# Four tables that place convolution and attention jobs among feed-forward chunks, laid out anew

## The chip, the cores and the metric

The kernel runs on one core of a Trainium2 chip. The metric is the device time of one launch in microseconds (us): the median of three runs before the change is 751.4, and the three lie between 750.59 and 752.95.

## The reference, cut to what matters

The input has 4 images of 96 channels and 56 x 56 pixels. Each goes through one transformer block:

```
x = x + conv_attention(layernorm over channels of x)
t = x as 3136 tokens of 96 channels
t = t + moe(layernorm(t))

conv_attention: value, query = depthwise 3x3 conv, stride 1;  key, off = the same, stride 2
   offset = w_off2 (gelu(layernorm(off)));  pos = tanh(offset + ref)
   sampled = value read bilinearly at pos (784 places, four neighbours each)
   out = (query^T key * scale) sampled  per head;   y = w_out out
moe: 4 experts, 96 -> 384 -> 96 with gelu, top 2 of a softmax gate:
   out = sum over experts of gate_e * (w2_e gelu(w1_e t + b1_e) + b2_e)
```

## The kernel before

**Two kinds of work share every engine.** The feed-forward part of an image is 84 chunks: 7 groups of 448 tokens, by 4 experts, by 3 slices of 128 hidden units. A chunk is, on PE, a first product in three passes (L762 to L764, fp32r split in high and low parts), a gelu on ACT (L1006), and a second product on PE (L746). PE issues the second product of chunk k-1 behind the first product of chunk k. There are two PSUM banks for first products, so PE can't be more than two chunks ahead of ACT. Three chunks make one output of an expert: DVE scales it by the gate (L1416, tile ye), and POOL adds it to the image (a sum). The first 76 sums are accumulating DMAs that POOL issues (L1480), and POOL waits before each until the sum before it has landed. The first 252 chunks (images 0 to 2) are spread between the convolution and attention jobs of images 1 to 3. The last 84 (image 3) run by themselves at the end, in another form (L782 to L797, L1015, L1443).

**The other kind are the jobs of the image ahead**, a long chain through all engines. For image b, in the order in which PE meets them:

- valT: transposes of the value convolution (L621). DVE has to be through with its nine value taps (L1133). ACT then writes the table of values to memory.
- xT: the next image's pixels to tokens (L529); keyT: the key convolution to samples (L566).
- pad: the next image, normalised, back to channels (L534 to L556). Ahead of it DVE takes the statistics and scales one part of the tokens (L1098), and ACT scales the rest (xn in its table, L831).
- kv (L632): products of keys and sampled values, in four quarters. DVE samples (L1335, L1338) from what POOL gathered from the table (L1469, two gathers for each of eight tiles). A DMA of this kind lands in the tile `big`.
- mix and y (L642, L662): the attention. DVE adds y to the image (L1354), and PE turns the sum to tokens again (x1T, L650).
- offT, offc, offs: the next image's offset convolution, from which DVE and ACT (tanh) derive the places of the gathers.
- x1c (L511): the normalised tokens back to channels, seven jobs. ACT takes the high part (L930), DVE the low part (L1369). Before them ACT scales three groups (x1n), and between them stand the softmax (exp, L939) and the gate (gateT).

DVE issues, in this order of an image: low parts of x1c, the offset normalisation, value and key and query taps, the statistics of the next image, the sampling, the masking of kv, the sums with y, the statistics of the tokens, the gate.

**The order on each engine is written out by hand in four tables.** `CHUNKS_AHEAD` says for each PE job how many chunks PE has to have issued before it. `GELUS_AHEAD` says the same of the gelus on ACT. `OUTPUTS_AHEAD` says how many outputs DVE has to have done at each of its turns (there is a turn before each convolution tap, each sampling quarter, and so on). `SUMS_AHEAD` says how many sums POOL has to have issued before the gathers of each tile. An engine works strictly in its own order: what is waiting holds up all that stands behind it on that engine. The tables are read through `Plan` at the calls `chunks_to`, `gelus_to`, `turn` and `add_outputs`; no other line decides the order.

Of the kernel before, what the change touches and what calls it, by code (L numbers as in the profile page):

```python
# [131 lines left out]

GELUS_AHEAD = [
    dict(x1n=(0, 0, 0), x1c=(0, 0, 0, 0, 3, 3, 4), exp=(0,), gateT=(3,), offT=(10, 10), offc=(16, 17), tanh=(19,)),
    dict(valT=(42, 42, 43, 43, 44, 44, 45), xT=(45, 46, 46, 47, 47, 48, 48), keyT=(49, 49), xn=(67, 69, 69),
         pad=(69, 70, 70, 71, 71, 72), mix=(73, 73, 74, 74), x1T=(74, 74, 74, 74, 74, 74, 75), offT=(75, 76),
         x1n=(78, 80, 82), x1c=(80, 81, 83, 84, 86, 86, 87), exp=(81,), gateT=(86,), offc=(93, 94), tanh=(95,)),
    dict(valT=(118, 118, 119, 119, 120, 120, 121), xT=(121, 122, 122, 123, 123, 124, 124), keyT=(125, 125),
         xn=(143, 144, 145), pad=(145, 146, 146, 147, 147, 148), mix=(151, 151, 152, 152),
         x1T=(152, 152, 152, 152, 152, 152, 153), offT=(153, 154), x1n=(156, 158, 160),  # L140
         x1c=(158, 159, 161, 162, 164, 164, 165), exp=(159,), gateT=(164,), offc=(172, 173), tanh=(175,)),
    dict(valT=(198, 198, 199, 199, 200, 200, 201), keyT=(204, 204), mix=(233, 233, 234, 234),
         x1T=(234, 234, 234, 234, 234, 234, 235), x1n=(239, 241, 243), x1c=(241, 242, 245, 245, 249, 249, 250),
         exp=(243,), gateT=(249,)),
]
# [1392 lines left out]
```

## Time and profile before

| | |
|---|---|
| runs | 750.59, 751.40, 752.95 us; median 751.4 |
| span of the profiled execution, first to last instruction | 749.4 us |
| what lies around the span, by the median | 2.0 us |
| PE busy | 707.8 us, 94% |
| DVE busy | 582.8 us, 78% |
| ACT busy | 384.5 us, 51% |
| POOL busy | 216.9 us, 29% |
| mean granted TensorE clock | 0.985 |

The span has four stages. Up to 130 us image 0 goes through convolution and attention with no chunks. From there to 637.7 us the 252 chunks alternate with the jobs of images 1 to 3. From 637.7 to about 742 us the last 84 chunks run alone, and the rest is the end of the last sums and stores. Matmul ends are modelled, so a busy PE isn't a PE at its peak: the distance between the starts of two chunks says more than the busy time. A wait is the number in square brackets at the end of a row, with what ended it.

### The profile page before, as it was taken

What the parts mean: (1) busy time and instruction counts of PE and PEld (TensorE: products, weight loads), DVE (VectorE), ACT (ScalarE), POOL (GpSimd) and SP (SyncE); (2) the same over time, 40 slices, a digit from 0 to 9 for tenths busy, and PEclk for the clock granted to TensorE, in tenths of its full rate; (3) what the DMA queues carried; (4) which work ended last, traced back from release to release, by engine and by line L of the source; (5) the groups of instructions that cost most, each with busy time, mean ns of one, the idle gap of its engine ahead of it and who ended that gap; (6) DMA issues with size and microseconds to landing.
All of it is one profiled execution on the core that took longest, in us unless ns stands there. A gap on an engine that the chain in (4) does not pass through costs nothing.

```text
span 749.4 us, 9619 instructions
## 1 busy us (share of the span) xinstructions
PE 707.8 (94%) x3186; PEld 495.8 (66%) x3186; DVE 582.8 (78%) x1511; ACT 384.5 (51%) x722; POOL 216.9 (29%) x184
## 2 busy tenths in 40 slices
PE   5798999799999999999999999999998999999996
PEld 5556566566676666556767566666664665788884
DVE  4889648899999858699999477899975275677774
ACT  2314124744464614744556218545542256899995
POOL 4001700012128610111168201222285121344443
PEclk9998999799999999999999999999999999999999
DMA  8007200044464530345654422435645201121111
GB/s 195 9 0 198 53 9 1 7 98 86 89 185 115 98 56 10 68 103 119 155 129 83 86 48 46 82 80 101 190 102 109 35 20 49 47 69 51 66 47 37
DMA packets 29697, 58.66 MB, mean 78 GB/s; under 512 B 6224, under 2 KB 20176, under 8 KB 29360
## 3 DMA queue, kind: packets, MB, share of 16 engines
q0 software_dynamic: 11584, 17.90, 15.4%
q1 hardware_dynamic: 14336, 32.59, 14.7%
q10 hardware_dynamic: 3728, 7.55, 3.3%
q8 instruction: 26, 0.43, 0.2%
q14 instruction: 23, 0.19, 0.1%
HBM read 30.30 MB, written 14.65 MB: 60 GB/s over the span
## 4 chain that ended last, share of the span: by engine, by line
PE 56%; DVE 19%; DMA 7%; ACT 6%; POOL 5%; issue 5%; POOLq 0%; ACTq 0%
PE py L746 9%; PE pd L662 8%; PE ph L578 7%; DVE val L1133 6%; POOL big L1469 4%; DMA xbuf<-ye 4%; DVE query L1133 3%; PE pa L650 3%; PE pa L529 2%; PE ph L762 2%; PE ph L782 2%; PE ph L784 2%; PE ph L763 2%; PE ph L783 2%; PE ph L764 2%
## 5 line engine op out<-in xcount | busy, mean ns | idle before, releaser
L746 PE MATMUL py<-hid,w 128*96 128x448 f32 x504 | 234.4, 546 | 11.5 <-ACT hid L1006 8.7
L1006 ACT ACTIVATE hid<-ph,b 128x448 f32<-128x448 f32 x252 | 158.9, 632 | 148.1 <-PE ph L764 144.8
L762 PE MATMUL ph<-x_hi,w_hi 96*128 96x448 f32 x252 | 164.4, 653 | 0.0
L1480 POOL DMA_DIRECT2D xbuf<-ye x76 | 66.6, 877 | 327.2 <-DMA xbuf<-ye 163.2
L1469 POOL DMA_INDIRECT big<-value_table,rows x64 | 87.8, 1372 | 90.5 <-DVE rows L1193 56.5
L746 PEld LDWEIGHTS py<-hid,w 128*96 128x96 f32 x504 | 81.6, 165 | 31.2 <-ACT hid L1006 12.6
L763 PE MATMUL ph<-x_lo,w_hi 96*128 96x448 f32 x252 | 93.5, 371 | 0.0
L764 PE MATMUL ph<-x_hi,w_lo 96*128 96x448 f32 x252 | 92.8, 368 | 0.0
L1482 POOL TENSOR_TENSOR xbuf<-xbuf,ye 96x448 f32<-96x448 f32 x36 | 53.9, 1497 | 102.6 <-DVE ye L1416 99.9
L1416 DVE SCALAR_TENSOR_TENSOR ye<-py,b,gate_all 96x448 f32<-96x448 f32 x112 | 75.3, 674 | 9.3 <-PE py L746 7.3
L1443 DVE TENSOR_TENSOR hid_lo<-hid,hid_hi 128x448 fp32r<-128x448 f32 x84 | 59.7, 710 | 27.3 <-ACT hid L1015 27.1
L1133 DVE SCALAR_TENSOR_TENSOR query<-xpad,conv_w,query 128x784 f32<-128x784 f32 x80 | 78.3, 1027 | 0.5
L1133 DVE SCALAR_TENSOR_TENSOR val<-xpad,conv_w,val 128x784 f32<-128x784 f32 x80 | 78.3, 1026 | 0.4
L762 PEld LDWEIGHTS ph<-x_hi,w_hi 96*128 96x128 f32 x252 | 48.3, 192 | 41.1 <-issue 39.7
L763 PEld LDWEIGHTS ph<-x_lo,w_hi 96*128 96x128 f32 x252 | 48.8, 194 | 35.6 <-issue 35.0
L662 PE MATMUL pd<-query,mix_area 128*96 128x392 f32 x192 | 67.2, 493 | 0.0
L1015 ACT ACTIVATE hid_hi<-ph,b 128x448 fp32r<-128x448 f32 x84 | 53.3, 634 | 6.9 <-PE ph L784 1.7
L1015 ACT ACTIVATE hid<-ph,b 128x448 f32<-128x448 f32 x84 | 52.5, 625 | 0.0
L826 ACT ACTIVATE big<-pa 112x400 f32<-112x400 f32 x28 | 14.0, 502 | 70.6 <-PE pa L650 70.6
L764 PEld LDWEIGHTS ph<-x_hi,w_lo 96*128 96x128 f32 x252 | 47.9, 190 | 3.3
L662 PEld LDWEIGHTS pd<-query,mix_area 128*96 128x96 f32 x192 | 29.6, 164 | 23.9 <-issue 23.9
L1354 DVE TENSOR_TENSOR xbuf<-pd,xbuf 96x392 f32<-96x392 f32 x32 | 17.9, 560 | 32.8 <-PE pd L662 32.5
(165 smaller groups left out, 1081.2 us busy)
## 6 DMA issues: line engine op xcount, KB each, us to landing
gate_all<-gate_rows SPq DMA_DIRECT2D x56, 336.0 KB, 3.5
xbuf<-ye POOLq DMA_DIRECT2D x76, 168.0 KB, 3.4
value_table<-valT ACTq DMA_DIRECT2D x6, 1176.0 KB, 8.9
out<-xbuf SPq DMA_DIRECT2D x28, 168.0 KB, 2.0
xbuf<-in_x SPq DMA_DIRECT2D x3, 1176.0 KB, 10.1
value_table<-valT SPq DMA_DIRECT2D x2, 672.0 KB, 5.3
big<-value_table,rows POOLq DMA_INDIRECT x64, 2.8
value_table<-valT SPq DMA_DIRECT2D x2, 504.0 KB, 5.0
```

The costliest lines, as they stand in the source:

```text
L662: last = nc.tensor.matmul(bank[0:C, 0:YPIX], mix[:, q, i, :], query[:, i, h * YPIX:(h + 1) * YPIX], start=(i == 0), stop=(i == BLOCKS - 1))
L746: nc.tensor.matmul(py[e % 2][0:C, 0:GPIX], w2[:, c, :], hid[:, k % 3, :], start=(j == 0), stop=(j == CPE - 1)).then_inc(hid_used, 1)
L762: nc.tensor.matmul(bank, w1_hi[:, cols], xh(b, g), start=True, stop=False)
L763: nc.tensor.matmul(bank, w1_hi[:, cols], xl(b, g), start=False, stop=False)
L764: nc.tensor.matmul(bank, w1_lo[:, cols], xh(b, g), start=False, stop=True).then_inc(hid_full, 1)
L1006: nc.scalar.activation(hid[:, k % 3, :], ph[k % 2][:, 0:GPIX], ACT.Gelu, bias=b1[:, k % NCH:k % NCH + 1]).then_inc(hid_act, 1)
L1015: nc.scalar.activation(dst[:, k % 3, :], ph[k % 2][:, 0:GPIX], ACT.Gelu, bias=b1[:, k % NCH:k % NCH + 1]).then_inc(ready, 1)
L1133: ins = v.scalar_tensor_tensor(to, src, w, to, ALU.mult, ALU.add)
L1416: v.scalar_tensor_tensor(ye[0:C, e, :], py[e % 2][0:C, 0:GPIX], b2[:, e:e + 1], gate_all[0:C, e, :], ALU.add, ALU.mult).then_inc(ye_ready, 1)
L1443: v.tensor_tensor(hid_lo[:, m % 2, :], hid[:, k % 3, :], hid_hi[:, k % 3, :].bitcast(f32), ALU.subtract).then_inc(hid_lo_ready, 1)
L1469: p.indirect_dma_start(got[:, tile, r, :, :].rearrange("p a c -> p (a c)"), None, table, bass.IndirectOffsetOnAxis(ap=rows[:, r, tile:tile ...
L1480: pool.dma_start(to, ye[0:C, e, :], accum_op=ALU.add).then_inc(ye_summed, 16)
```

## The change

All four tables get new numbers. Nothing else differs: the same instructions, with the same operands, in other positions relative to each other. The order of jobs among themselves is unchanged on every engine.

```diff
@@ CHUNKS_AHEAD, one dict for each image @@
-    dict(x1c=(0, 0, 0, 0, 3, 3, 4), gateT=(3,), offT=(10, 10), offc=(16, 16), offs=(18,)),
-    dict(valT=(42, 42, 43, 43, 44, 44, 45), xT=(45, 46, 46, 47, 47, 48, 48), keyT=(49, 49),
-         pad=(69, 69, 70, 71, 71, 72), kv=(72, 72, 73, 73), mix=(73, 73, 74, 74), y=(74, 74, 74, 74, 74, 74, 74, 74),
-         x1T=(74, 74, 74, 74, 74, 74, 75), offT=(75, 76), x1c=(80, 80, 81, 82, 86, 86, 87), gateT=(86,), offc=(93, 93),
-         offs=(95,)),
-    dict(valT=(118, 118, 119, 119, 120, 120, 121), xT=(121, 122, 122, 123, 123, 124, 124), keyT=(125, 125),
-         pad=(145, 145, 146, 147, 147, 148), kv=(148, 148, 151, 151), mix=(151, 151, 152, 152),
...
-         x1c=(158, 158, 159, 160, 164, 164, 165), gateT=(164,), offc=(172, 172), offs=(174,)),
-    dict(valT=(198, 198, 199, 199, 200, 200, 201), keyT=(204, 204), kv=(222, 226, 233, 233), mix=(233, 233, 234, 234),
...
-         x1c=(241, 241, 243, 243, 249, 249, 250), gateT=(249,)),
+    dict(x1c=(0, 0, 0, 2, 5, 5, 6), gateT=(4,), offT=(12, 12), offc=(18, 18), offs=(19,)),
+    dict(valT=(44, 44, 45, 45, 46, 46, 47), xT=(47, 47, 48, 48, 49, 49, 50), keyT=(50, 51), pad=(69, 69, 70, 70, 70,
+         71), kv=(71, 71, 72, 72), mix=(72, 72, 73, 73), y=(73, 73, 73, 73, 73, 73, 73, 73), x1T=(73, 73, 73, 73, 73,
+         73, 74), offT=(74, 75), x1c=(78, 78, 79, 80, 84, 84, 85), gateT=(84,), offc=(92, 92), offs=(93,)),
+    dict(valT=(117, 117, 118, 118, 119, 119, 120), xT=(120, 120, 121, 121, 122, 122, 123), keyT=(123, 124), pad=(142,
+         142, 143, 143, 143, 144), kv=(144, 144, 146, 146), mix=(146, 146, 147, 147), y=(147, 147, 147, 147, 147, 147,
+         147, 147), x1T=(147, 147, 147, 147, 147, 147, 148), offT=(148, 149), x1c=(152, 152, 153, 154, 159, 159, 160),
+         gateT=(159,), offc=(167, 167), offs=(168,)),
+    dict(valT=(192, 192, 193, 193, 194, 194, 195), keyT=(198, 198), kv=(216, 219, 229, 229), mix=(229, 229, 230, 230),
...
+         243, 243, 244), gateT=(243,)),
@@ GELUS_AHEAD, from images 0 and 3 @@
-    dict(x1n=(0, 0, 0), x1c=(0, 0, 0, 0, 3, 3, 4), exp=(0,), gateT=(3,), offT=(10, 10), offc=(16, 17), tanh=(19,)),
-         x1T=(234, 234, 234, 234, 234, 234, 235), x1n=(239, 241, 243), x1c=(241, 242, 245, 245, 249, 249, 250),
-         exp=(243,), gateT=(249,)),
+    dict(x1n=(0, 0, 2), x1c=(0, 0, 2, 2, 5, 5, 6), exp=(0,), gateT=(4,), offT=(12, 12), offc=(18, 18), tanh=(21,)),
+         230, 230, 231), x1n=(234, 236, 239), x1c=(236, 237, 239, 240, 243, 243, 244), exp=(237,), gateT=(243,)),
@@ SUMS_AHEAD @@
-              (15, 16, 17, 17, 18, 18, 19, 20),
-              (40, 41, 42, 42, 43, 43, 44, 44),
-              (67, 68, 69, 70, 70, 71, 71, 72)]
+              (17, 18, 19, 19, 20, 21, 22, 22),
+              (41, 41, 42, 43, 44, 45, 46, 47),
+              (67, 68, 69, 70, 71, 71, 72, 72)]
```

`OUTPUTS_AHEAD` (one number for each of DVE's 105 turns, 76 for the last image) moves by up to three outputs. At the turn before query tap 6 of image 1 it has 17 before and after; behind the scaling of the next image's tokens (L1098) it has 22 before and after. At query tap 5 of image 2 it has 41 before and after. For image 3 it has 67 outputs at the last key tap before, and at query tap 5 after. At the last turns of the four images it has 6, 32, 58, 84 before and 7, 31, 56, 81 after.

## Rows read from the trace of the kernel before

**Rows 1.** Busy time by stretch (`a:b length`, busy (instructions) of each engine, granted clock, DMA share, GB/s).
```profile
130.00:145.00 15.00, 10.30 (x50) 7.86 (x51) 12.79 (x50) 11.59 (x26) 0.00 (x0) 0.69 0.00 0
165.00:195.00 30.00, 30.00 (x128) 20.16 (x126) 29.45 (x61) 14.64 (x24) 5.52 (x7) 1.00 0.49 100
612.00:640.00 28.00, 25.63 (x105) 16.25 (x103) 15.85 (x40) 19.08 (x40) 8.19 (x6) 0.94 0.10 35
```
**Rows 2.** Timeline (start, duration, instruction, [wait before it]), PE, two chunks in a row.
```profile
333.70 0.71 PE L762 MATMUL ph<-x_hi,w_hi 96*128 96x448 f32 x1
335.06 0.72 PE L762 MATMUL ph<-x_hi,w_hi 96*128 96x448 f32 x1
```
**Rows 3.** Timeline, PE: the second product of chunk 0 waits for its gelu.
```profile
142.39 1.81 PE L746 MATMUL py<-hid,w 128*96 128x448 f32 x2 [1.50 <-ACT hid L1006]
```
**Rows 4.** Timeline, the first chunks: ACT's third scaling and the gelus' table load.
```profile
138.38 1.16 ACT L831 ACTIVATE big<-big,rstd 112x96 f32<-112x96 f32 x4
...
140.41 1.28 ACT L1006 ACT_TABLE_LOAD   x1
```
**Rows 5.** Timeline, ACT, scaling ahead of pad in images 1 and 2.
```profile
247.72 1.17 ACT L831 ACTIVATE xT<-xT,rstd 112x96 f32<-112x96 f32 x4 [0.43 <-DVE rstd L1072]
...
402.93 1.16 ACT L831 ACTIVATE xT<-xT,rstd 112x96 f32<-112x96 f32 x4
```
**Rows 6.** Timeline, POOL, gathers of image 1: the first, a slow, a fast, the last.
```profile
223.27 1.38 POOL L1469 DMA_INDIRECT big<-value_table,rows  x1 [6.28 <-DMA value_table<-valT]
224.95 4.01 POOL L1469 DMA_INDIRECT big<-value_table,rows  x1 [0.30 <-issue]
...
239.12 0.97 POOL L1469 DMA_INDIRECT big<-value_table,rows  x1 [0.30 <-issue]
...
255.89 0.96 POOL L1469 DMA_INDIRECT big<-value_table,rows  x1 [0.30 <-issue]
```
**Rows 7.** The page's DMA issues: the sums (count, KB of one, median us from issue to landing).
```profile
xbuf<-ye POOLq DMA_DIRECT2D x76, 168.0 KB, 3.4
```
**Rows 8.** Timeline, DVE, image 1: the 17th output, the last query tap, the sampling's wait.
```profile
228.00 0.67 DVE L1416 SCALAR_TENSOR_TENSOR ye<-py,b,gate_all 96x448 f32<-96x448 f32 x1
...
234.98 2.92 DVE L1133 SCALAR_TENSOR_TENSOR query<-xpad,conv_w,query 128x784 f32<-128x784 f32 x3
...
258.58 0.27 DVE L1335 TENSOR_SCALAR key_area<-big,w 98x96 f32<-98x96 f32 x1 [2.29 <-DMA big<-value_table,rows]
258.76 1.46 DVE L1338 SCALAR_TENSOR_TENSOR key_area<-big,w,key_area 98x96 f32<-98x96 f32 x6
```
**Rows 9.** Timeline, PE, third and fourth kv job of image 1.
```profile
261.61 2.74 PE L632 MATMUL pd<-keyT,key_area 98*96 98x384 f32 x8
```
**Rows 10.** Timeline, POOL, gathers of image 2: the sum before, the first, the last.
```profile
380.56 0.79 POOL L1480 DMA_DIRECT2D xbuf<-ye  x1 [10.32 <-DMA xbuf<-ye]
381.65 1.79 POOL L1469 DMA_INDIRECT big<-value_table,rows  x1 [0.30 <-issue]
...
412.88 0.97 POOL L1469 DMA_INDIRECT big<-value_table,rows  x1 [0.30 <-issue]
```
**Rows 11.** Timeline, PE, third and fourth kv job of image 2.
```profile
420.89 2.79 PE L632 MATMUL pd<-keyT,key_area 98*96 98x384 f32 x8 [1.06 <-DVE kv_area L1348]
```
**Rows 12.** Timeline, image 3: POOL's first and last gather.
```profile
540.33 1.07 POOL L1469 DMA_INDIRECT big<-value_table,rows  x1 [9.22 <-DMA value_table<-valT]
...
572.01 0.97 POOL L1469 DMA_INDIRECT big<-value_table,rows  x1 [0.30 <-issue]
```
**Rows 13.** Timeline, image 3: DVE's output at query tap 5, PE's wait before the third kv.
```profile
540.17 0.67 DVE L1416 SCALAR_TENSOR_TENSOR ye<-py,b,gate_all 96x448 f32<-96x448 f32 x1
...
577.15 0.96 PE L746 MATMUL py<-hid,w 128*96 128x448 f32 x2 [1.88 <-DVE ye L1416]
```
**Rows 14.** Timeline, PE, the wait at the softmax: images 1 and 3.
```profile
305.07 0.99 PE L746 MATMUL py<-hid,w 128*96 128x448 f32 x2 [1.62 <-ACT hid L1006]
...
623.74 1.75 PE L746 MATMUL py<-hid,w 128*96 128x448 f32 x2 [1.80 <-ACT hid L1006]
```

More of the change, by code:

```diff
@@ L118 @@
 CHUNKS_AHEAD = [
-    dict(x1c=(0, 0, 0, 0, 3, 3, 4), gateT=(3,), offT=(10, 10), offc=(16, 16), offs=(18,)),
-    dict(valT=(42, 42, 43, 43, 44, 44, 45), xT=(45, 46, 46, 47, 47, 48, 48), keyT=(49, 49),
-         pad=(69, 69, 70, 71, 71, 72), kv=(72, 72, 73, 73), mix=(73, 73, 74, 74), y=(74, 74, 74, 74, 74, 74, 74, 74),
-         x1T=(74, 74, 74, 74, 74, 74, 75), offT=(75, 76), x1c=(80, 80, 81, 82, 86, 86, 87), gateT=(86,), offc=(93, 93),
-         offs=(95,)),
-    dict(valT=(118, 118, 119, 119, 120, 120, 121), xT=(121, 122, 122, 123, 123, 124, 124), keyT=(125, 125),
-         pad=(145, 145, 146, 147, 147, 148), kv=(148, 148, 151, 151), mix=(151, 151, 152, 152),
-         y=(152, 152, 152, 152, 152, 152, 152, 152), x1T=(152, 152, 152, 152, 152, 152, 153), offT=(153, 154),
-         x1c=(158, 158, 159, 160, 164, 164, 165), gateT=(164,), offc=(172, 172), offs=(174,)),
@@ L128 @@
-    dict(valT=(198, 198, 199, 199, 200, 200, 201), keyT=(204, 204), kv=(222, 226, 233, 233), mix=(233, 233, 234, 234),
-         y=(234, 234, 234, 234, 234, 234, 234, 234), x1T=(234, 234, 234, 234, 234, 234, 235),
-         x1c=(241, 241, 243, 243, 249, 249, 250), gateT=(249,)),
+    dict(x1c=(0, 0, 0, 2, 5, 5, 6), gateT=(4,), offT=(12, 12), offc=(18, 18), offs=(19,)),
+    dict(valT=(44, 44, 45, 45, 46, 46, 47), xT=(47, 47, 48, 48, 49, 49, 50), keyT=(50, 51), pad=(69, 69, 70, 70, 70,
+         71), kv=(71, 71, 72, 72), mix=(72, 72, 73, 73), y=(73, 73, 73, 73, 73, 73, 73, 73), x1T=(73, 73, 73, 73, 73,
+         73, 74), offT=(74, 75), x1c=(78, 78, 79, 80, 84, 84, 85), gateT=(84,), offc=(92, 92), offs=(93,)),
@@ new lines @@
+    dict(valT=(117, 117, 118, 118, 119, 119, 120), xT=(120, 120, 121, 121, 122, 122, 123), keyT=(123, 124), pad=(142,
[3 more added lines that the diff above has]
+    dict(valT=(192, 192, 193, 193, 194, 194, 195), keyT=(198, 198), kv=(216, 219, 229, 229), mix=(229, 229, 230, 230),
+         y=(230, 230, 230, 230, 230, 230, 230, 230), x1T=(230, 230, 230, 230, 230, 230, 231), x1c=(236, 236, 237, 238,
+         243, 243, 244), gateT=(243,)),
@@ L131 @@
 ]
 GELUS_AHEAD = [
-    dict(x1n=(0, 0, 0), x1c=(0, 0, 0, 0, 3, 3, 4), exp=(0,), gateT=(3,), offT=(10, 10), offc=(16, 17), tanh=(19,)),
[L135 to L141, printed above, removed]
@@ L142 @@
-    dict(valT=(198, 198, 199, 199, 200, 200, 201), keyT=(204, 204), mix=(233, 233, 234, 234),
-         x1T=(234, 234, 234, 234, 234, 234, 235), x1n=(239, 241, 243), x1c=(241, 242, 245, 245, 249, 249, 250),
-         exp=(243,), gateT=(249,)),
+    dict(x1n=(0, 0, 2), x1c=(0, 0, 2, 2, 5, 5, 6), exp=(0,), gateT=(4,), offT=(12, 12), offc=(18, 18), tanh=(21,)),
+    dict(valT=(44, 44, 45, 45, 46, 46, 47), xT=(47, 47, 48, 48, 49, 49, 50), keyT=(50, 51), xn=(67, 68, 69), pad=(69,
+         69, 70, 70, 70, 71), mix=(72, 72, 73, 73), x1T=(73, 73, 73, 73, 73, 73, 74), offT=(74, 75), x1n=(77, 78, 81),
+         x1c=(78, 79, 81, 82, 84, 84, 85), exp=(79,), gateT=(84,), offc=(92, 92), tanh=(95,)),
@@ new lines @@
+    dict(valT=(117, 117, 118, 118, 119, 119, 120), xT=(120, 120, 121, 121, 122, 122, 123), keyT=(123, 124), xn=(140,
+         141, 142), pad=(142, 142, 143, 143, 143, 144), mix=(146, 146, 147, 147), x1T=(147, 147, 147, 147, 147, 147,
+         148), offT=(148, 149), x1n=(151, 152, 155), x1c=(152, 153, 155, 156, 159, 159, 160), exp=(153,), gateT=(159,),
+         offc=(167, 167), tanh=(170,)),
+    dict(valT=(192, 192, 193, 193, 194, 194, 195), keyT=(198, 198), mix=(229, 229, 230, 230), x1T=(230, 230, 230, 230,
+         230, 230, 231), x1n=(234, 236, 239), x1c=(236, 237, 239, 240, 243, 243, 244), exp=(237,), gateT=(243,)),
```

24 rows, old and new, of the table OUTPUTS_AHEAD are left out of this document.

## The prediction

> **What bounds the kernel now.** I read the page first: PE is busy 94% of the span. Then busy time by stretch: from 145 us on PE is nearly always occupied, and DVE as much as PE wherever it works on convolution taps, 29.45 of 30 us in one stretch [rows 1]. Then PE's timeline, by the distance between the starts of two chunks: 335.06 - 333.70 = 1.36 us where nothing interferes [rows 2]. That distance is the price of a chunk, wherever a table puts it. All 252 chunks and all jobs have to be issued before the last stage, which the change doesn't touch. So the time moves by one thing: the sum of PE's waits up to the last stage. Last I read who ends those waits.
>
> There are two kinds of stretch. Where PE leads (kv to y, the x1c jobs), DVE waits for PE, and a chunk taken out makes DVE's chain start sooner. Where DVE or POOL leads (from x1c to pad, and the gathers before the third kv job), PE must be kept busy until they are through, and a chunk taken out there becomes 1.36 us of waiting. So I go stretch by stretch: chunks before and after, and whether the releaser moves.
>
> **The change part by part** (plus is more PE waiting).
>
> a) *Image 0's x1c jobs.* ACT now does gelus 0 and 1 ahead of its third scaling. The table load that precedes the gelus began at 140.41; it can begin where that scaling did, at 138.38 [rows 4], 2.0 us earlier. PE's second product of chunk 0 then follows about 2 us before 142.39, where it had waited 1.50 [rows 3]. Against it, jobs 5 to 7 come two chunks later and DVE with them, which may return 1.3. For it, the clock: this stretch ran at a granted 0.69 [rows 1], and a PE that waits less may be back at the upper level sooner, worth up to 0.8 more. Bounds -2.8 and -0.7; I take -1.9, near the two rows.
>
> b) *Image 1, x1c to pad.* DVE's chain has the same outputs as before up to the statistics. PE has 69 - 3 = 66 chunks from the fifth x1c job to pad; now 69 - 5 = 64. There was no slack: ACT already waited 0.43 for DVE's statistics [rows 5], with a gelu queued behind that scaling and PE behind the gelu. Two chunks are 2.7 of waiting. Bounds 1.4 (one of them absorbed) and 2.7; I take 2.7.
>
> c) *Image 1, the gathers.* Before: 15 sums, then the gathers from 223.27 to the last issue at 255.89 + 0.96 = 256.85 [rows 6]. Now 17 sums come first, and the 17th needs DVE's 17th output, which stands at the same turn as before and ends at 228.67 [rows 8]. With one POOL issue of 1 us between, the first gather starts near 229.8, 6.5 late. The 33.6 us from first to last gather held 16 gathers and 5 sums. At the fast rate (0.97 + 0.30 [rows 6]) these 21 take 26.7; the other 6.9 us are slow ones like the 4.01 us gather, all before 239, while DVE runs query taps (the last ends at 237.9 [rows 8]). Starting at 229.8, 9 of those 15.5 us are left, so 4.0 slow. The end: 229.8 + 26.7 + 4.0 = 260.5, 3.6 late. The last quarter's sampling waited 2.29 for its gather and ended at 260.22 [rows 8]; PE came at 261.61 without waiting [rows 9], 1.4 of slack, and now comes a chunk earlier. So the wait is 3.6 + 1.4 - 1.4 = 3.6. Bounds: 0 (no slow gather at all: an end at 256.5) and 5 (each sum also held up by the landing of the one before, 3.4 [rows 7]). I take 2.8, nearer the slow row.
>
> The Trainium skill, SBUF — State Buffer, section "Who interferes with whom", says that a DVE instruction with two SBUF inputs, as a tap is, holds up a GpSimd instruction that reads SBUF. The trace agrees as far as it goes: 4.01 beside taps, 0.97 behind them. By that rule alone c comes to 3.6; if instead the first gathers were slow wherever they stand, to 6.5.
>
> d) *Image 2, x1c to pad.* From the seventh x1c job 145 - 87 = 58 chunks, now 142 - 85 = 57, with 18 outputs on DVE in both. ACT found the statistics just ready there, without a wait [rows 5]: 1.4 less 0.3 of slack is 1.1. Bounds 0 and 1.4.
>
> e) *Image 2, pad to the third kv.* 151 - 145 = 6 chunks, now 146 - 142 = 4: 2.7. PE already waited there, 1.06 [rows 11]. POOL now has 41 sums ahead of the first gather, not 40, and six among the gathers, not four. The sum at 380.56 stood just before the first gather at 381.65 [rows 10]; one more has to wait for its landing, 3.4 [rows 7], so the gathers start about 3.9 late. From 381.65 to 413.85 are 32.2 us; 20 issues at the fast rate are 25.4, 6.8 slow. Starting at 385.5 about 4.8 slow remain, and 22 issues take 28.0: an end at 418.3, 4.4 late. Together 2.7 + 4.4 = 7.1. Bounds: -1.1 (the extra sum at once and no slow gather, an end at 410) and 7.5. I take 5.0. Behind the waiting kv job stand mix, all of y and every later chunk.
>
> f) *Image 3.* One chunk less up to valT, partly paid by one output less on DVE: 0.4 (0 to 1). The first gather needs 67 sums as before, but DVE now has its 67th output at query tap 5, at 540.17 to 540.84 [rows 13]: the first gather near 542.1 rather than 540.33 [rows 12], the last about 1 late. Against it, 37 chunks rather than 35 lie between valT and the third kv, 2.7, and PE's wait there, 1.88 at the end [rows 13], is covered: -1.4 (-2 to 1).
>
> g) *Image 3's softmax.* On all images PE waits while ACT loads a table for exp and another for gelu: 1.62 in image 1 [rows 14]. In image 3 the third scaling (1.16) lay between the loads too, PE waited 1.80 and came back at half clock, the second product taking 1.75 where 0.99 is usual [rows 14]; the stretch shows 0.94 [rows 1]. Two gelus now stand between exp and that scaling, as in images 1 and 2: -2.0 (-2.4 to -1.5).
>
> h) *The rest.* Eight chunks, not two, follow the last x1c job. They cost their 1.36 each as anywhere, so nothing; they only would have covered waits of image 3's tail that g has counted. valT and keyT moves within b and d cost nothing while the taps behind them set the time; without that cover they cost 1.36 a chunk.
>
> Sum: -1.9 + 2.7 + 2.8 + 1.1 + 5.0 + 0.4 - 1.4 - 2.0 = +6.7. The profiled span of 749.4 would become 756.1; the median of the runs lies 2.0 above that span, so 751.4 + 6.7 = 758.1.
>
> **The rivals.**
>
> *The gathers aren't late (faster).* POOL's slow issues belong to the taps, and gathers that start behind them may run at 0.97 each; then c and e vanish. With a at -2.8, b at 2.7, d at 0.5, f at -1.4 and g at -2.4 this gives -3.4: 748.0. It decides if the last gathers of images 1 and 2 issue no later than 256.85 and, in e, 2.7 earlier than 413.85. For it: the 0.97 rows. Against: the outputs that the sums wait for.
>
> *Half late (no change).* c and e at 1.0 each: -1.9 + 2.7 + 1.0 + 1.1 + 1.0 + 0.4 - 1.4 - 2.0 = +0.9: 752.3.
>
> *The clock falls as well.* A PE wait of 5 to 7 us in image 2 can be followed by a stretch at the lower of the two levels (1.2 rather than 2.4 GHz), as after PE's waits at 130 to 145 us: 0.69 over 15 us is 4.6 us of clock lost [rows 1]. About two thirds of that on top: 761. Against it: waits up to 1.9 us show none but in g. The Trainium skill, TensorE: Matmul & The Clock Gate, section "Part 1: The HAM clock gate", has the throttled state as the default that activity releases; by that rule a long wait in e is paid twice.
>
> **How the numbers follow.** The forecast has a chance of 0.50, the clock rival 0.17, half late 0.14, the gathers on time 0.19. A measurement of this kernel tells about 0.3%, 2.3 us, from no change. Slower by more: 0.50 + 0.17 = 0.67; within: 0.14; faster: 0.19. The likeliest case's own range is 754.5 to 761. The 8 in 10 range reaches to the clock rival with c and e near their upper ends, 764.5, and to the faster rival's own time, 747.5, where half of it is left out.
>
> **What would show it.** In the new profile: ACT's wait before its scaling ahead of pad in image 1 grows from 0.43 to about 2 or more (b). The first gather of image 1 starts near 230, behind the 17th output; the last quarter's sampling waits for it, and PE for the sampling, some 3 us (c). The third kv job of image 2 waits 5 us or more (e). The wait for gelu at the last softmax falls to about 1.6, at full clock (g). The forecast is wrong if the third kv jobs of images 1 and 2 wait no longer than before: then POOL's order wasn't the bound, and PE's lost chunks were covered by a DVE chain that starts sooner than I have it.

## The result and the profile after

The changed kernel takes 784.4 us (median of 4 runs, 783.45 to 785.33) against 751.0 for the kernel before on the same chip: 1.0427 times as long, 95% interval 1.0396 to 1.0457. The forecast was 758.1 with a range up to 764.5. The direction was right; the size was +33.4 instead of +6.7. The span of the profiled execution grew by 33.1, from 749.4 to 782.5. Some executions of any of these programs fall into a state that is a per cent or two slower; ratios and intervals leave them out, medians and ranges of runs do not.

The page of the changed kernel: busy time of the engines, granted clock in 40 slices of 19.6 us, and the chain that ended last, by line. (In the code after the change all lines of these engines stand two lower: L746 is L744, L632 is L630, L1480 is L1478, L1416 is L1414.)
```profile
PE 724.4 (93%) x3186; PEld 504.9 (65%) x3186; DVE 583.3 (75%) x1511; ACT 384.8 (49%) x722; POOL 205.3 (26%) x184
...
PEclk9998999799999799999999599999989999999998
...
DMA xbuf<-ye 19%; PE pd L660 8%; PE ph L576 6%; PE py L744 6%; DVE val L1131 4%; POOL big L1467 4%; PE pd L630 3%; PE pa L648 3%; PE pa L527 2%; PE ph L780 2%; PE ph L782 2%; PE ph L781 2%; PE py L792 2%; PE py L795 2%; PE py L793 2%
```
DVE and ACT did the same work as before. PE is "busy" 16.6 us longer with the same instructions, so part of it ran slowly: the clock row has three dips (7 in slice 14, 5 in slice 23, 8 in slice 30) that the kernel before doesn't have. The landing of sums, `xbuf<-ye`, is 19% of the last chain; it was 4%.

To find where the 33 us arise I compared the start of the same PE job in both traces and added 1.365 us, the distance of two chunks [rows 2], for each chunk that the changed kernel had not yet issued there. The difference is delay at equal work:

| PE job | before, us (chunks) | after, us (chunks) | delay, us |
|---|---|---|---|
| first pad job in image 0's part (no chunks yet) | 128.58 (0) | 128.02 (0) | -0.6 |
| a valT job, image 1 | 206.60 (43) | 211.38 (45) | +2.1 |
| first kv, image 1 | 257.64 (72) | 262.10 (71) | +5.8 |
| third kv, image 1 | 261.61 (73) | 271.16 (72) | +10.9 |
| y, image 1 | 268.21 (74) | 279.88 (73) | +13.0 |
| a valT job, image 2 | 364.37 (120) | 373.72 (119) | +10.7 |
| first kv, image 2 | 412.96 (148) | 422.82 (144) | +15.3 |
| third kv, image 2 | 420.89 (151) | 436.42 (146) | +22.4 |
| tokens behind y, image 2 | 433.46 (152) | 456.98 (147) | +30.4 |
| a valT job, image 3 | 525.78 (201) | 548.00 (195) | +30.4 |
| first kv, image 3 | 556.91 (222) | 584.06 (216) | +35.3 |
| third kv, image 3 | 577.95 (233) | 607.01 (229) | +34.5 |
| last stage | 637.71 (252) | 670.91 (252) | +33.2 |

The big steps are at the third kv jobs of images 1 and 2 and the first of image 3. PE's timeline there (start, duration, instruction, wait), to be held against [rows 9, 11]:
```profile
271.16 4.12 PE L630 MATMUL pd<-keyT,key_area 98*96 98x384 f32 x6 [4.91 <-DVE kv_area L1346]
...
427.40 0.92 PE L744 MATMUL py<-hid,w 128*96 128x448 f32 x2
436.42 4.12 PE L630 MATMUL pd<-keyT,key_area 98*96 98x384 f32 x6 [8.10 <-DVE kv_area L1346]
...
584.06 2.88 PE L630 MATMUL pd<-keyT,key_area 98*96 98x384 f32 x4 [5.06 <-DVE key_area L1336]
```
No wait became 4.91, 1.06 became 8.10, and the first kv of image 3, which had waited 0.44, waits 5.06. The kv_area mask named as the releaser stands on DVE behind the sampling, and the sampling waited for gathers, in image 2 for the last one:
```profile
434.17 0.27 DVE L1333 TENSOR_SCALAR key_area<-big,w 98x96 f32<-98x96 f32 x1 [3.48 <-DMA big<-value_table,rows]
```
POOL's timeline, images 1 and 2, against [rows 6, 10]:
```profile
227.10 0.79 POOL L1478 DMA_DIRECT2D xbuf<-ye  x1 [9.97 <-DVE ye L1414]
233.49 0.79 POOL L1478 DMA_DIRECT2D xbuf<-ye  x1 [5.60 <-DVE ye L1414]
234.58 2.38 POOL L1467 DMA_INDIRECT big<-value_table,rows  x1 [0.30 <-issue]
...
266.35 0.96 POOL L1467 DMA_INDIRECT big<-value_table,rows  x1 [0.30 <-issue]
...
377.99 0.79 POOL L1478 DMA_DIRECT2D xbuf<-ye  x1 [4.49 <-DMA xbuf<-ye]
388.76 0.79 POOL L1478 DMA_DIRECT2D xbuf<-ye  x1 [9.98 <-DMA xbuf<-ye]
392.62 0.79 POOL L1478 DMA_DIRECT2D xbuf<-ye  x1 [3.07 <-DMA xbuf<-ye]
396.46 0.79 POOL L1478 DMA_DIRECT2D xbuf<-ye  x1 [3.06 <-DMA xbuf<-ye]
397.55 3.17 POOL L1467 DMA_INDIRECT big<-value_table,rows  x1 [0.30 <-issue]
```
Three sums wait one behind the other before image 2's first gather, where one did. One of the two more is the table's number, 41 for 40; the other is that POOL had issued 38 sums before the wait, and not 39. The sum at 388.76 waits 9.98 because the one before it, issued at 377.99, lands at 388.23 only: the value table is being written meanwhile (376.8 to 388.6), as before 380.56 in [rows 10]. The next two cost 3.9 us each.

The clock falls to the lower level during each long wait, and PE runs at that level behind it. Busy time by stretch, columns as in [rows 1], granted clock third from the end:
```profile
432.00:453.00 21.00, 16.58 (x43) 10.75 (x44) 5.52 (x15) 2.28 (x5) 1.56 (x2) 0.51 0.17 41
436.42:453.00 16.58, 16.58 (x43) 10.72 (x44) 3.27 (x7) 2.28 (x5) 0.95 (x1) 0.50 0.18 43
268.00:275.00 7.00, 3.84 (x6) 1.81 (x7) 3.13 (x10) 0.00 (x0) 0.29 (x1) 0.54 0.24 38
155.90:159.30 3.40, 3.40 (x8) 2.08 (x7) 2.39 (x7) 0.85 (x2) 0.00 (x0) 0.50 0.68 152
```
The last row is one of three shorter stretches at 0.50 that the kernel before does not have. They last 3.4 us each, from 155.9, 254.9 and 415.3, behind waits of PE of 1.89, 2.09 and 1.95 us in the parts of images 0, 1 and 2. If work at half clock takes twice as long, each costs up to 1.7 us (an estimate from its length).

### The profile page after: what moved, and what is told of

It reads as the page before. It is cut to its first block, busy times and chain, and to the rows that moved or that the text cites. A ratio compares the mean times of both kernels' runs of the same rounds, so it can differ in the third digit from the quotient of the medians.

```text
span 782.5 us, 9621 instructions
## 1 busy us (share of the span) xinstructions
PE 724.4 (93%) x3186; PEld 504.9 (65%) x3186; DVE 583.3 (75%) x1511; ACT 384.8 (49%) x722; POOL 205.3 (26%) x184
## 4 chain that ended last, share of the span: by engine, by line
PE 49%; DMA 20%; DVE 14%; issue 6%; ACT 5%; POOL 5%; POOLq 0%; DVEq 0%; ACTq 0%
DMA xbuf<-ye 19%; PE pd L660 8%; PE ph L576 6%; PE py L744 6%; DVE val L1131 4%; POOL big L1467 4%; PE pd L630 3%; PE pa L648 3%; PE pa L527 2%; PE ph L780 2%; PE ph L782 2%; PE ph L781 2%; PE py L792 2%; PE py L795 2%; PE py L793 2%
## 5 line engine op out<-in xcount | busy, mean ns | idle before, releaser
L744 PE MATMUL py<-hid,w 128*96 128x448 f32 x504 | 237.0, 552 | 9.8 <-ACT hid L1004 7.5
L1478 POOL DMA_DIRECT2D xbuf<-ye x76 | 64.1, 843 | 380.3 <-DVE ye L1414 237.1
L744 PEld LDWEIGHTS py<-hid,w 128*96 128x96 f32 x504 | 82.5, 166 | 29.1 <-ACT hid L1004 11.7
L1467 POOL DMA_INDIRECT big<-value_table,rows x64 | 78.8, 1232 | 76.1 <-DVE rows L1191 57.0
L1414 DVE SCALAR_TENSOR_TENSOR ye<-py,b,gate_all 96x448 f32<-96x448 f32 x112 | 75.4, 674 | 18.3 <-PE py L744 14.0
L1480 POOL TENSOR_TENSOR xbuf<-xbuf,ye 96x448 f32<-96x448 f32 x36 | 53.9, 1496 | 109.7 <-DVE ye L1414 109.4
L660 PE MATMUL pd<-query,mix_area 128*96 128x392 f32 x192 | 68.9, 503 | 0.0
L630 PE MATMUL pd<-keyT,key_area 98*96 98x384 f32 x64 | 28.2, 595 | 18.1 <-DVE kv_area L1346 13.0
## 6 DMA issues: line engine op xcount, KB each, us to landing
xbuf<-in_x SPq DMA_DIRECT2D x3, 1176.0 KB, 10.3
```

The costliest lines, as they stand in the source:

```text
L660: last = nc.tensor.matmul(bank[0:C, 0:YPIX], mix[:, q, i, :], query[:, i, h * YPIX:(h + 1) * YPIX], start=(i == 0), stop=(i == BLOCKS - 1))
L744: nc.tensor.matmul(py[e % 2][0:C, 0:GPIX], w2[:, c, :], hid[:, k % 3, :], start=(j == 0), stop=(j == CPE - 1)).then_inc(hid_used, 1)
L1414: v.scalar_tensor_tensor(ye[0:C, e, :], py[e % 2][0:C, 0:GPIX], b2[:, e:e + 1], gate_all[0:C, e, :], ALU.add, ALU.mult).then_inc(ye_ready, 1)
L1467: p.indirect_dma_start(got[:, tile, r, :, :].rearrange("p a c -> p (a c)"), None, table, bass.IndirectOffsetOnAxis(ap=rows[:, r, tile:tile ...
L1478: pool.dma_start(to, ye[0:C, e, :], accum_op=ALU.add).then_inc(ye_summed, 16)
```

## The experiments

Ratios are against the kernel before, run beside each of these on the same chip. Its medians there were 751.3 to 752.0, and its single runs scattered more than in the first comparison (748 to 759), so differences under 2 us are not told apart by the times alone. A trace shows one execution, and not always a typical one: those of e1 (761.7 us), e3 (754.0) and e13 (771.0) are some 5 us faster than the medians.

### POOL's order, both ways

e1: after, with the old `SUMS_AHEAD`. e2: before, with the new one.
```diff
# e1, on the changed kernel (e2 is the reverse, on the kernel before)
-              (17, 18, 19, 19, 20, 21, 22, 22),
-              (41, 41, 42, 43, 44, 45, 46, 47),
-              (67, 68, 69, 70, 71, 71, 72, 72)]
+              (15, 16, 17, 17, 18, 18, 19, 20),
+              (40, 41, 42, 42, 43, 43, 44, 44),
+              (67, 68, 69, 70, 70, 71, 71, 72)]
```


> The changed kernel with one table put back, the sums ahead of each gather (15 to 20, 40 to 44, 67 to 72 as before); chunks, gelus and outputs stay as changed. Theory 1, the order of sums and gathers on POOL is the cause: the first gather of image 1 moves from 234.6 to about 227, that of image 2 from 397.6 to about 393.5, PE's wait before the third kv job of image 2 falls from 9 us to 3 or less, and the time from 784.4 to 760 to 767. Rival 2, too few chunks ahead of pad and kv: PE runs out of chunks at the same place whatever POOL's order, 778 to 785. Rival 3, the outputs stand later on DVE and the sums wait for them: the sums still wait as long, 775 to 783.

> The kernel before with only the table of sums ahead of each gather taken from the change (17 to 22, 41 to 47). Theory 1: the gathers of images 1 and 2 start 4 to 8 us late and end 4 to 9 us late, PE waits at the third kv jobs of both; 760 to 772. Rival 2 (chunks) and rival 3 (outputs), each alone the cause: 750 to 754.

e1 took 767.0 us (1.0234, 1.0174 to 1.0293), e2 768.9 (1.0258, 1.0203 to 1.0312). So the order of sums alone is worth about 17 of the 33 us, in either direction, and the other tables 15; the intervals reach some 4 us to either side. PE at the third kv jobs of images 1 and 2, and at the first of image 3, in e1:
```profile
267.03 2.74 PE L630 MATMUL pd<-keyT,key_area 98*96 98x384 f32 x8
...
422.49 1.82 PE L630 MATMUL pd<-keyT,key_area 98*96 98x384 f32 x5 [0.37 <-DVE kv_area L1346]
...
561.99 2.88 PE L630 MATMUL pd<-keyT,key_area 98*96 98x384 f32 x4 [4.90 <-DVE key_area L1336]
```
and at the two third kv jobs in e2:
```profile
264.33 5.40 PE L632 MATMUL pd<-keyT,key_area 98*96 98x384 f32 x8 [4.27 <-DVE kv_area L1348]
...
435.93 5.39 PE L632 MATMUL pd<-keyT,key_area 98*96 98x384 f32 x8 [4.33 <-DVE kv_area L1348]
```
The waits of images 1 and 2 go and come with this one table, so chunks or outputs alone (rivals 2 and 3) do not make them. Sums alone make 4.33 of image 2's 8.10, though: the rest comes only together with the other tables. In image 3, whose numbers hardly differ, the wait of 5 us stays in e1; e5 below shows why. My guess of where e1's first gathers would start was off (229.9 and 388.1 rather than 227 and 393.5).

### Fewer sums than either kernel

e5: after, starting at 14, 38 and 65. e7: before, starting at 14, 38 and 66.
```diff
# e7, on the kernel before
-              (15, 16, 17, 17, 18, 18, 19, 20),
-              (40, 41, 42, 42, 43, 43, 44, 44),
-              (67, 68, 69, 70, 70, 71, 71, 72)]
+              (14, 15, 16, 17, 17, 18, 18, 19),
+              (38, 39, 40, 40, 41, 42, 43, 43),
+              (66, 67, 68, 69, 70, 70, 71, 71)]
```


> The changed kernel with fewer sums ahead of the gathers than either kernel has: image 1 from 14, image 2 from 38, image 3 from 65, later ones among the gathers; chunks, gelus and outputs as changed. Theory 1 with its refined form (a sum issued while the value table is being written waits some 10 us for the landing of the one before, and every sum ahead of the first gather then costs 3 to 4 us more): the first gathers follow the landing of the table, 2 to 6 us sooner than with the old sums, the 4.9 us wait before the first kv job of image 3 shrinks to under 1.5, and the time goes to 759 to 764 (the changed kernel with the old sums: 767.0). Rival: what is left over the kernel before comes from the chunks ahead of pad and the outputs alone, POOL's order has nothing left to give, 766 to 769. Second rival: DVE's outputs wait for the sums put off, slower than 769.

> The kernel before with one or two sums fewer ahead of the gathers (14, 38, 66 rather than 15, 40, 67). If POOL's order sets the waits at the third kv jobs of images 2 and 3 (1.06 and 1.88), they shrink: -1 to -3, 748.5 to 750.5. If those waits hang on DVE or the table's landing alone: within 1 us of before. If the sums put off hold up outputs on DVE, and so PE: +1 to +4.

Both lost: e5 775.4 us (1.0298, 1.0251 to 1.0345), e7 762.0 (1.0139, 1.0099 to 1.0178). DVE and PE in image 2 of e7:
```profile
396.23 0.68 DVE L1416 SCALAR_TENSOR_TENSOR ye<-py,b,gate_all 96x448 f32<-96x448 f32 x1 [4.36 <-DMA xbuf<-ye]
405.51 0.68 DVE L1416 SCALAR_TENSOR_TENSOR ye<-py,b,gate_all 96x448 f32<-96x448 f32 x1 [5.12 <-DMA xbuf<-ye]
```
```profile
406.34 1.78 PE L746 MATMUL py<-hid,w 128*96 128x448 f32 x2 [4.99 <-DVE ye L1416]
```
A sum put off keeps one of DVE's output buffers: DVE waits for its landing and PE for DVE. So the numbers are bounded on both sides, and my refined form of theory 1, that fewer is better, was wrong (its second rival holds).

One part of it came true. In e5, with 65 sums rather than 67 ahead of image 3's first gather, PE's wait at the first kv of image 3 is 0.82 us where the changed kernel and e1 have 5:
```profile
578.82 1.53 PE L630 MATMUL pd<-keyT,key_area 98*96 98x384 f32 x4 [0.82 <-DVE key_area L1336]
```
The change issues valT of image 3 behind 192 to 195 chunks, before it was 198 to 201. At three chunks an output, that is 64 or 65 outputs rather than 66 or 67, but the table of sums still asks for 67.

### Which sums cost it: ahead of the first gather, or among the gathers

e10 and e11 change only image 2's row of the kernel before and load the front; e14 keeps the front and takes the change's later numbers.
```diff
-              (40, 41, 42, 42, 43, 43, 44, 44),
+              (41, 41, 42, 42, 43, 43, 44, 44),   # e10
+              (43, 43, 43, 43, 43, 43, 44, 44),   # e11
+              (40, 40, 42, 43, 44, 45, 46, 47),   # e14
```


> The kernel before with one more sum, 41 rather than 40, ahead of image 2's first gather, nothing else. My term in step e: the gathers start 3.9 and end 4.4 us late; the third kv job waits 3 to 5 us longer: 754.5 to 757. If that sum waits some 10 us while the value table is written: 758 to 763. If it hides behind the table's landing: 751 to 752.

> The kernel before with 43 rather than 40 sums ahead of image 2's first gather (and 44 to 45 later). Each sum waits for the landing of the one before and for its output: 3 to 4 us a sum, gathers 9 to 13 us late, PE's wait at the third kv job 8 us or more and a stretch at half clock behind it: 763 to 772. Rival, sums are issued at 1 us each: 753 to 756. If a long wait of PE doesn't bring half clock, 759 to 762.

> The kernel before with image 2's first gather behind 40 sums as before, and then the change's numbers (42, 43, 44, 45, 46, 47 rather than 42, 42, 43, 43, 44, 44): three more sums between first and last gather. If sums among the gathers cost their issue alone (1.28 us each): the last gather ends 3 to 4 us late, 752 to 755. If each also waits for the landing or the output before it (about 4 us a sum, as in the changed kernel): 4 to 8 us late and a half-clock stretch behind the third kv job, 755 to 763. If only sums ahead of the first gather matter: 751 to 752.

e10: 753.8 us (1.0015, 0.9986 to 1.0044), no difference that can be told. e11: 756.6 (1.0076, 1.0050 to 1.0102), far under theory 1's 763 to 772. e14: 766.0 (1.0139, 1.0090 to 1.0188), the dearest of the three, with runs from 758 to 770 (the trace is of one of 768.1). POOL in e11 and then in e14:
```profile
393.23 0.79 POOL L1480 DMA_DIRECT2D xbuf<-ye  x1 [3.68 <-DMA xbuf<-ye]
394.33 1.34 POOL L1469 DMA_INDIRECT big<-value_table,rows  x1 [0.30 <-issue]
...
419.10 0.97 POOL L1480 DMA_DIRECT2D xbuf<-ye  x1
```
```profile
401.04 0.83 POOL L1480 DMA_DIRECT2D xbuf<-ye  x1 [3.08 <-DMA xbuf<-ye]
402.18 1.07 POOL L1469 DMA_INDIRECT big<-value_table,rows  x1 [0.31 <-issue]
403.55 1.00 POOL L1469 DMA_INDIRECT big<-value_table,rows  x1 [0.30 <-issue]
405.04 0.95 POOL L1480 DMA_DIRECT2D xbuf<-ye  x1 [0.50 <-issue]
...
409.12 0.95 POOL L1480 DMA_DIRECT2D xbuf<-ye  x1 [0.51 <-DMA xbuf<-ye]
...
413.22 0.94 POOL L1480 DMA_DIRECT2D xbuf<-ye  x1 [0.52 <-DMA xbuf<-ye]
```
In e11 the gathers start 12.7 us later than in [rows 10], but nearly all sums are then behind them, most gathers run through at 1.27 us each, and POOL is done with them by 419.10, 5.2 late. Of that, 4.3 are older than the sums (the run's trace has that delay at valT of image 2 already, 2.4 of it before the first chunk, and 5.4 at the third kv): in this execution three more sums ahead of the first gather cost about 1 us. By the times e11 costs 4 to 8 us, so other executions must lose more; where is open. In e14 the first gather starts at 384.62, but a sum stands behind every second gather, and two sums are never closer than 4.0 us, since each waits for the landing of the one before: seven of them pace the last gather to 426.7. The delay grows from 2.4 at valT to 10.3 at the third kv, where PE waits, and to 17.0 behind y, at half clock.
```profile
431.23 4.08 PE L632 MATMUL pd<-keyT,key_area 98*96 98x384 f32 x8 [3.87 <-DVE kv_area L1348]
```
The kernel before, e10 and e11 all have 44 sums ahead of the last gather, e14 has 47. What counts most is how many sums stand ahead of the **last** gather, at 4 us each in a chain of their own; at the same 44, more of them ahead of the first gather cost less. All 47 ahead of the first gather were not tried.

### Filling the waits

e13: the changed kernel with spare matmuls ahead of the three long waits.
```diff
+FILL = {(1, 2): 20, (2, 2): 38, (3, 0): 20}
...
                     before(q)
+                    spare = act_bank(b, "mix", 0) if (b, q) in FILL else None
+                    for _ in range(FILL.get((b, q), 0)):
+                        nc.tensor.matmul(spare[:, 0:448], w1_hi[:, 0:128], w1_hi[:, 0:448], start=True, stop=True)
                     pe.wait_ge(sampled, b * QUARTERS + q + 1)
```


> The changed kernel, with 20, 38 and 20 spare matmuls (w1_hi against itself, 448 columns, into a free bank that the mix overwrites; about 0.2 us each) put on PE ahead of its waits for the samples at the third kv jobs of images 1 and 2 and the first kv job of image 3 (5.1, 9.0 and 6.0 us of idle PE). All dependencies stay. If the half-clock stretches behind these waits follow from PE's idleness, they go and the time falls by about 10 of the 33: 772 to 776. If the clock falls for another reason, or the work behind the waits is bound by DVE and not by PE: 783 to 786.

776.3 us (1.0357, 1.0293 to 1.0422), 8 less than the changed kernel; the execution traced took 771.0. PE at image 2's third kv, and the stretch behind it:
```profile
422.36 8.21 PE L630 MATMUL pa<-w_hi 96*128 96x448 f32 x38
431.74 2.47 PE L634 MATMUL pd<-keyT,key_area 98*96 98x384 f32 x7 [1.17 <-DVE kv_area L1350]
```
```profile
431.00:452.00 21.00, 20.27 (x96) 12.97 (x97) 12.86 (x37) 3.78 (x8) 0.94 (x1) 1.00 0.13 33
```
The same dependencies, the clock at 1.00 instead of 0.51. Of the half-clock stretches of the changed kernel those behind the three filled waits are gone, and those at 155.9 and 254.9, whose waits were not filled, are still there (at 154.4 and 253.4). The one at 415.3 is gone too: PE's wait there is 0.58 instead of 1.95. By the equal-work delay, from the third kv to the tokens behind y nothing is lost any more (17.7 at both) where 8.0 were; in image 1 the 2.1 are gone too (9.4 at both). So PE's idleness brought the lower level.

### Image 0, and what is left without it

e3: image 0's rows of all tables alone. e4: images 0 and 1. e8: only the gelus moved ahead of the scaling. e15: only the fifth to seventh x1c job, the gate and the offsets two chunks later. e9: the change with old sums and old image 0.
```diff
-    dict(x1c=(0, 0, 0, 0, 3, 3, 4), gateT=(3,), offT=(10, 10), offc=(16, 16), offs=(18,)),
+    dict(x1c=(0, 0, 0, 2, 3, 3, 4), gateT=(3,), offT=(10, 10), offc=(16, 16), offs=(18,)),   # e8
+    dict(x1c=(0, 0, 0, 0, 5, 5, 6), gateT=(5,), offT=(12, 12), offc=(16, 16), offs=(18,)),   # e15
...
-    dict(x1n=(0, 0, 0), x1c=(0, 0, 0, 0, 3, 3, 4), exp=(0,), gateT=(3,), offT=(10, 10), offc=(16, 17), tanh=(19,)),
+    dict(x1n=(0, 0, 2), x1c=(0, 0, 2, 2, 3, 3, 4), exp=(0,), gateT=(3,), offT=(10, 10), offc=(16, 17), tanh=(19,)),   # e8
+    dict(x1n=(0, 0, 0), x1c=(0, 0, 0, 0, 5, 5, 6), exp=(0,), gateT=(5,), offT=(12, 12), offc=(16, 17), tanh=(19,)),   # e15
```


> The kernel before with the rows of image 0 alone taken from the change, in all tables. My step a: PE waits less at image 0's softmax, -1.9, 749.1. By the trace of the changed kernel, in which chunk 6 starts 0.8 us earlier but the chunks behind offT 1.9 later with a second stretch at half clock, +2, 753.

> The kernel before with the rows of images 0 and 1 taken from the change, images 2 and 3 as before. If the delay arises where the trace shows it, 13 us are there by the first x1c job of image 1 and stay: 761 to 765, with image 2's third kv job waiting no more than before. If images 2 and 3 can absorb it in chains that PE waits for anyway, 752 to 757. If the loss of image 2 follows from the late start of image 1, and not from image 2's rows, 770 to 780.

> The kernel before with only the first half of step a: gelus 0 and 1 ahead of ACT's third and fourth scaling in image 0 (and so two chunks ahead of the fourth x1c job on PE); jobs 5 to 7, the offsets and all other tables stay. Step a as I costed it: PE is 1.9 to 2.8 earlier by job 4, and all of it stays: 748 to 749.5. Rival: DVE, which gets its split later, pays it back as a wait for ye or for the query taps by the values of image 1, as in the run with all rows of image 0 (-2.8 at chunk 3, +4.3 at chunk 42): 752 to 756.

> The kernel before with only image 0's fifth to seventh x1c job, the gate and the offsets' transposes two chunks later (gelus, outputs and sums as before). My step a priced this part at +1.3 at most. By the traces of the kernels with image 0's new rows, DVE waits for these jobs, comes out 2 to 5 us late, and is busy without a gap up to pad of image 1, so that all of it returns: 754 to 757.

> The changed kernel with the old sums and with image 0's rows as before too: what is left of the change are the chunks, gelus and outputs of images 1 to 3. With image 0's new rows the run with the old sums took 767.0 and was 6.8 us late by the second kv job of image 1. If that comes from image 0's later jobs (5.2 us lost between the x1c jobs and the values in the run with image 0's rows alone): nothing lost by pad of image 1, 757 to 760 in all. If image 1's own rows cost their 4 us of it (values at the same turn but the statistics later): 761 to 764. Where the chunk count between the fifth x1c job and pad decides (66 again here, as before): 757 to 760 too, and the wait ahead of pad is under 1 us.

e3: 759.6 us (1.0080, 1.0041 to 1.0118), with runs from 752 to 766. e4: 763.3 (1.0190, 1.0118 to 1.0262): the delay of images 0 and 1 stays, as its first case had it, and image 2's third kv doesn't suffer from it. e8: 752.1 (1.0008, 0.9978 to 1.0037): of the 1.9 to 2.8 its trace keeps 0.7 at the offsets' transposes. e15: 761.8 (1.0133, 1.0095 to 1.0171), worse than expected. DVE in e15:
```profile
151.16 0.62 DVE L1369 TENSOR_TENSOR x_lo<-pd,x_hi 96x448 fp32r<-96x448 f32 x1 [3.99 <-ACT x_hi L930]
...
164.31 0.68 DVE L1416 SCALAR_TENSOR_TENSOR ye<-py,b,gate_all 96x448 f32<-96x448 f32 x1 [2.91 <-issue]
...
167.82 1.38 DVE L1160 BATCH_NORM_STATS2 st<-kv_area 98x6 f32<-98x96 f32 x8 [2.83 <-ACT kv_area L866]
```
DVE loses 9.7 us in three waits where it lost 1.7 in the kernel before, and the delay of PE is 7.6 us by valT of image 1. With all of image 0's rows from the change, the gelus among them (e3), it is 4.8.

e9: 759.2 us (1.0096, 1.0063 to 1.0129), so image 0's rows carry 7.8 of the 15.4 us that e1 is over the kernel before. The rest is in the rows of images 1 to 3: up to the first kv of image 1 the trace loses 3.5 us where e1's loses 6.6, and a wait ahead of the pad in image 1's part is still there. ACT's scaling and the DVE outputs before it in e9:
```profile
248.24 1.17 ACT L829 ACTIVATE xT<-xT,rstd 112x96 f32<-112x96 f32 x4 [2.11 <-DVE rstd L1070]
```
```profile
176.36 0.68 DVE L1414 SCALAR_TENSOR_TENSOR ye<-py,b,gate_all 96x448 f32<-96x448 f32 x1 [0.51 <-PE py L744]
180.45 0.68 DVE L1414 SCALAR_TENSOR_TENSOR ye<-py,b,gate_all 96x448 f32<-96x448 f32 x1 [0.58 <-PE py L744]
...
188.63 0.68 DVE L1414 SCALAR_TENSOR_TENSOR ye<-py,b,gate_all 96x448 f32<-96x448 f32 x1 [0.51 <-PE py L744]
```
With 66 chunks ahead of pad, as before, ACT waits 2.11 instead of 0.43 [rows 5]. The three waits of DVE, for outputs that now stand a turn sooner than PE has their chunks, sum to 1.6, which is about the difference. That they cause it was not tried apart.

### The pieces meant to gain

e6: before, with image 3's softmax as in the change. e12: e6 and e8 together. e16: e6, with 8 spare matmuls ahead of each of PE's three waits in image 0's softmax.
```diff
-         ... x1c=(241, 241, 243, 243, 249, 249, 250), gateT=(249,)),
+         ... x1c=(241, 241, 242, 243, 248, 248, 249), gateT=(248,)),   # e6, CHUNKS_AHEAD
-         ... x1n=(239, 241, 243), x1c=(241, 242, 245, 245, 249, 249, 250), exp=(243,), gateT=(249,)),
+         ... x1n=(239, 241, 244), x1c=(241, 242, 244, 245, 248, 248, 249), exp=(242,), gateT=(248,)),   # e6, GELUS_AHEAD
```


> The kernel before with image 3's softmax laid out as in the change (two gelus between exp and the third scaling, as images 1 and 2 have it), nothing else. My step g: the 1.80 us wait for gelu and the half clock behind it go, -2.0, 749.5. By the traces of the changed kernel and of the one with the old sums, in which the same stretch gains 0.6 to 1.3: -1. Rival, the time is only moved to the wait for the last jobs: 0.

> The kernel before with two pieces of the change alone: gelus 0 and 1 ahead of the third scaling in image 0, and image 3's softmax with two gelus behind exp. Steps a and g as I costed them: -3.9, 747.5. By the two runs of the pieces (752.1 and 750.3 against 751.9): -1 to -2, 750 to 751. If what PE saves early comes back as waits for DVE: 0.

> A version meant to beat both: the kernel before with image 3's softmax laid out as in the change, and with 8 spare matmuls (448 columns, into a free bank) ahead of each of PE's three waits in image 0's softmax (1.54, 1.63 and 1.50 us), behind which the kernel before runs at half clock from 135.7 to 146.0. If that half clock follows from PE's idleness, the chunks between 142 and 146 run at full clock: 2 to 3 us, and 1.5 from image 3: 747 to 749. If ACT sets the time there whatever PE's clock: 750 to 751.

e6: 750.3 us (0.9980, 0.9955 to 1.0005). e12: 751.3 (0.9989, 0.9957 to 1.0021). e16: 750.0 (0.9973, 0.9935 to 1.0012), the lowest median of all, 2.0 under the kernel before, with an interval that still reaches 1. In e6 image 3's stretch, and in e16 image 0's, run at full clock (0.94 in [rows 1]; 0.50 at 136 to 142 in the kernel before):
```profile
612.00:640.00 28.00, 25.68 (x113) 16.90 (x112) 16.39 (x42) 20.85 (x43) 7.74 (x6) 1.00 0.15 52
```
```profile
136.00:142.00 6.00, 5.55 (x36) 4.96 (x34) 4.37 (x18) 5.69 (x15) 0.00 (x0) 1.00 0.00 0
142.00:148.00 6.00, 4.26 (x22) 2.72 (x21) 5.66 (x20) 3.99 (x7) 0.00 (x0) 1.00 0.03 8
```
At full clock through image 0's softmax, PE is 1.2 us earlier by valT of image 1, although 10.2 us at half clock are gone. In the kernel before ACT is busy 5.94 of the 6 us from 136 there, so it is likely ACT that sets the time, and half clock costs less than its length suggests.

## Why the prediction was wrong in size

Delays by my steps, from the table above (the 2.3 us that come back between y of image 1 and valT of image 2 are counted in d, and "clock" counts only the stretches behind the two third kv jobs):

| step | predicted | measured |
|---|---|---|
| a and b, image 0's jobs, up to the first kv of image 1 | +0.8 | +6.4 |
| c, image 1's gathers | +2.8 | +7.2: wait 5.1, clock 2.1 |
| d, image 2 up to the first kv | +1.1 | +2.3 |
| e, image 2's third kv | +5.0 | +15.0: wait 7.0, clock 8.0 |
| f, image 3 up to the third kv | -1.0 | +4.2 |
| g, image 3's softmax | -2.0 | -1.3 |
| sum | +6.7 | +33.8 |

Of the 27 us that the forecast lacks, 10.1 are the clock behind the two third kv jobs, 5.6 a and b, 5.2 f, 4.3 the waits of c and e, and 1.9 d and g.

**a failed in its counterweight.** I gave DVE's two later chunks "may return 1.3". They returned more than all that was gained: e15 alone costs 10 us by the times, and image 0's rows as a whole (e3) 6. DVE waits for the jobs, and then has no gap up to pad, so PE must wait for it. The row that says so stood in front of me: DVE busy 29.45 of 30 us [rows 1]. Delay handed to a full engine isn't absorbed. PE's first wait of this kind is 1.89 at 154.67, where the kernel before waits 0.50, and the half clock from 155.9 follows it.

**b had its mark, but not its reason.** ACT's wait grew from 0.43 to 2.40, as forecast, and PE's behind it is 2.09; the half clock from 254.9 was not in the sum. e9 shows such a wait without the loss of chunks that I held responsible: there it seems to come from outputs placed a turn before PE has them. In the changed kernel DVE's lateness of about 5 us from image 0 comes on top. How much the 64 chunks themselves add was not separated.

**c and e had the right place, a term too small, and one left to a rival.** Without the change's sums the waits are gone (e1); with them alone they are there (e2). I priced sums among gathers at their issue, 1.27 us, and had gathers that start later run faster. From the first gather to the end of the last took 32.7 us in image 1 and 35.1 in image 2, where I had 30.7 and 32.8. (Image 1's first gather also came at 234.58 rather than near 229.8, because DVE's 17th output ended at 233.19 and not at 228.67. PE was about as late by then, so this did not add to its wait.) e14 shows the price: 4.0 us from sum to sum. My own upper bound in c named it ("each sum also held up by the landing"), and I took the lower price. In e the extra sum ahead of the first gather, which I took as the core of the step, is cheap by itself (e10). The Trainium skill, DMA: Bandwidth & Descriptors, section "Anatomy of one DMA — SWDGE (gpsimd) path", puts a DMA of this kind at 2.0 us fixed plus its bytes at 436 GB/s, an estimate of 2.4 us for 168 KB, most of it the wait for the write to be confirmed. The traces agree if the count starts behind the issue on POOL: 2.4 us at least, and 3.2 with the 0.8 of the issue. Beside the table's write a sum took 10.2, which the estimate does not have; there the measurement decides.

**The clock was a rival at 0.17, with two thirds of 4.6 us.** It cost 8.0 behind image 2's wait alone and 2.1 behind image 1's, and e13 took both away. I had set against it that waits up to 1.9 us show no lower level but in g; in the changed kernel waits of 1.89, 1.95 and 2.09 us each have 3.4 us of it behind them. The 4.6 us themselves were read from image 0's softmax, where e16 gains only 1.2 by full clock. The Trainium skill, TensorE: Matmul & The Clock Gate, section "HAM oscillation — how this bites in real kernels", describes a loop whose waits for DMAs throttle PE anew each time. The runs agree: 0.50 from 436.42, where image 2's wait ends, and 1.00 with the wait filled.

**f failed.** I followed the first gather and the third kv. The wait came at the first kv, 5.06, since the sums at 563.09 and 567.93 wait 9.54 and 4.05 for the landings before them, the first of which fell into the table's write. The kernel before issued its 67th at 530.32, also during that write, but none had to follow it. e1 has the same wait with the old sums, and e5 with 65 sums ahead hardly has it (0.82). So the step that failed is "67 sums as before": with fewer chunks ahead of valT, the last two of the 67 outputs come too late.

**g was right** in its mechanism: e6 waits 1.55 and stays at full clock; its trace gains 1.5 where I had 2.0. e6's time alone can't confirm it.

**The rival on the other side**, gathers on time behind the taps, fell in the change; e11 shows that it exists. There most gathers do run at 1.27 us each when they start late and hardly any sum stands among them.

By the times the parts add up: sums alone +17 (e2), everything else +15 (e1), together +33. By place they do not. From the first kv to the tokens behind y, e2's trace loses 12.5 us in image 1 and 5.8 in image 2; in the changed kernel the same steps, c and e, are 7.2 and 15.0.

One slip of the prediction changed nothing: the range's lower end, 747.5, is called the faster rival's own time, which is 748.0.
